# A Macaron block with tree-position attention: preparation moved out of the first rounds, into turns of 28 units, and a part of the lead given to GpSimd

## The reference

```python
q, k, v = heads(x @ Wq), heads(x @ Wk), heads(x @ Wv)        # 16 heads of 16
node_probs = softmax((x @ Wr) as (b, h, s, 4))
pos = cumsum(node_probs, axis=2) - node_probs                # in 0 .. 2047
cos, sin = tables at pos, linear between whole positions
cos_w, sin_w = sums over the 4 nodes of node_probs * cos, sin
q_r = q * cos_w + rotate_half(q) * sin_w                     # k_r likewise
scores = q_r k_r^T / 4 + log(node_probs node_probs^T + 1e-8), causal
out = softmax(scores) @ v @ Wo
```

## Time and profile before

| | |
|---|---|
| Three runs, median (lowest to highest) | 2910.24 us (2907.36 to 2912.67) |
| Profiled execution | 2896.46 us, span 2894.6 us |
| Feed-forward layer, then the lead | from 0 to 536.01 us of the span |
| Rounds 0 to 7 | 536.01 to 2529.75 us |
| Last projections, feed-forward layer | to 2894.6 us |

### The profile page before, as it was taken

One profiled execution on the slowest core, in us unless ns is written; L12 is line 12 of the kernel. 1 busy time (PEld: TensorE's weight loads), 2 busy tenths in 40 slices (PEclk: granted clock), 3 DMA queues, 4 the chain that ended last, 5 costly groups with the idle time before them and its releaser, 6 DMA issues. The chain is left out here.

```text
span 2894.6 us, 104325 instructions
## 1 busy us (share of the span) xinstructions
PE 2448.1 (85%) x45990; PEld 1896.7 (66%) x45990; DVE 1711.7 (59%) x3627; ACT 1702.9 (59%) x2174; POOL 997.9 (34%) x1497
## 2 busy tenths in 40 slices
PE   7298444587899999899999989999999999973885
PEld 4165222466788887778888777888877888841553
DVE  7732278788576567866566786666676111167431
ACT  6222123456677777667777766777776777662221
POOL 1188700334222224423222442222244222110787
PEclk9699776799999999999999999999999999986997
DMA  6555401221212112212111221211122111162565
GB/s 233 160 103 101 78 18 30 60 53 47 60 57 56 48 46 79 66 49 59 55 53 52 79 66 53 58 53 53 54 74 69 44 47 49 42 204 72 105 102 74
DMA packets 185109, 207.28 MB, mean 72 GB/s; under 512 B 35984, under 2 KB 151712, under 8 KB 184480
## 3 DMA queue, kind: packets, MB, share of 16 engines
q1 hardware_dynamic: 158880, 165.60, 19.3%
q0 software_dynamic: 24576, 34.10, 7.6%
q10 hardware_dynamic: 1152, 0.26, 0.0%
HBM read 131.68 MB, written 76.02 MB: 72 GB/s over the span
## 5 line engine op out<-in xcount | busy, mean ns | idle before, releaser
L1697 PEld LDWEIGHTS at_mix<-at_val,at_ew 128*64 128x64 f32 x34816 | 1223.7, 138 | 241.3 <-issue 36.0
L1281 ACT ACTIVATE at_ew<-at_ring 128x1024 f32<-128x1024 f32 (+1 forms) x1280 | 1124.7, 898 | 364.4 <-PE at_ring L1679 358.2
L1697 PE MATMUL at_mix<-at_val,at_ew 128*64 128x68 f32 x34816 | 1263.0, 224 | 44.7 <-DVE at_mixed L1543 28.7
L1679 PE MATMUL at_ring<-at_qT,at_kT 98*64 98x512 bf16 (+3 forms) x5120 | 698.9, 353 | 57.9 <-ACT at_ew L1281 35.8
L1202 POOL TENSOR_SCALAR_AFFINE_SELECT at_ew<-at_ew 128x256 f32<-128x256 f32 x512 | 294.3, 579 | 1074.2 <-ACT at_ew L1281 1073.5
L1543 DVE TENSOR_TENSOR at_mixed<-at_mix,at_prob 128x272 f32<-128x272 f32 x256 | 112.3, 439 | 440.4 <-PE at_mix L1697 439.1
L1679 PEld LDWEIGHTS at_ring<-at_qT,at_kT 98*64 98x64 bf16 x5120 | 228.5, 112 | 111.4 <-ACT at_ew L1281 47.6
L1224 POOL TENSOR_TENSOR at_val<-at_vo,at_val 128x256 f32<-128x256 f32 x384 | 267.4, 717 | 7.5
L344 POOL DMA_INDIRECT out_dram<-ffn_xn,ffn_idx_all x128 | 210.0, 1641 | 43.4 <-issue 35.0
L334 POOL DMA_INDIRECT ffn_xn<-table,ffn_idx_all x128 | 126.2, 986 | 278.4 <-DMA ffn_idx_all<-ffn_idx_hi 240.3
L1762 PE MATMUL at_side<-at_w_all,at_turned 128*64 128x512 f32 (+1 forms) x1024 | 197.8, 531 | 13.8 <-DVE at_bounded L1536 5.2
(11 more groups left out here) (243 smaller groups left out, 2727.1 us busy)
## 6 DMA issues: line engine op xcount, KB each, us to landing
table<-ffn_xn SPq DMA_DIRECT2D x32, 512.0 KB, 6.3
q_parts<-at_parts SPq DMA_DIRECT2D x64, 192.0 KB, 2.5
k_parts<-at_parts SPq DMA_DIRECT2D x64, 192.0 KB, 3.0
at_qT<-q_parts SPq DMA_DIRECT2D x128, 96.0 KB
at_kT<-k_parts SPq DMA_DIRECT2D x64, 192.0 KB
ffn_front<-in_L_attn_x_dram SPq DMA_DIRECT2D x16, 512.0 KB, 5.3
ffn_w_in<-in_L_ffn_w_dram SPq DMA_DIRECT2D x32, 256.0 KB, 3.6
at_xin<-out_dram SPq DMA_DIRECT2D x32, 256.0 KB, 6.0
```

The lines of the kernel that those rows point to most:

```text
L1281: act.activation(ew[u % NE_BUF][:, a:b], ring[u % 2][:, a:b], ACT.Exp).then_inc(s["exp_ready"], 1)
L1679: lastm = pe.matmul(ring[u % 2][h:h + HALF, at:at + (CH - t) * P], kT[q][:, kc + j * P + h:kc + j * P + h + HALF], qT[q][:, qc + t * P:qc ...
L1697: m = pe.matmul(mix[block_of[u] % 2][h:h + HALF, t * K * VW:(t + 1) * K * VW], ew[u % NE_BUF][:, col + h:col + h + HALF], val[q][:, tile0 ...
```

## The change

Round by round, turns are laid out anew: round 0 has four SHORT turns of 24 units; each second round has eight turns of 28 units (MID); the first rounds 2, 4 and 6 are one turn each without steps (BARE). Steps may stand at the same `at`, and VectorE's are cut into smaller ones. In MID turns ScalarE's copies stand at other distances from TensorE's steps than in LONG ones, and weighting runs without lag from 16 to 22 of a turn. Products and sums are made in quarters in MID turns. In the lead, GpSimd joins the halves and makes the product of the sine with g, and VectorE's statistics stand ahead of its positions. The rotated rows are turned by 8 transposes of whole tiles.

```diff
-    SHORT, LONG = 24, 40
-    N_SHORT = 4
+    SHORT, MID, BARE = 0, 1, 2
+    N_SHORT, N_MID = 4, 8
...
+    rounds = [first_unit[v] for v in range(V) if v == 0 or visits[v][1] != visits[v - 1][1]] + [U]
+    turns, m = [], 0
+    for r in range(len(rounds) - 1):
+        size = rounds[r + 1] - rounds[r]
+        count, kind = (N_SHORT, SHORT) if r == 0 else (N_MID, MID) if r % 2 else (1, BARE)
+        for n in range(count):
+            turns.append((rounds[r] + n * (size // count), size // count, kind, None if kind == BARE else m))
+            m += kind != BARE
...
+    STORE_AT = (20, 21, None)
...
-        BURST = 26
+        BURST, BURST_END = 16, 22
...
                 # GpSimd
-                    if at == (10 if short else 14) and new is not None:
+                    if at == (10, 12, None)[kind] and new is not None:
...
+                def join_halves(t):
+                    pool.wait_ge(s["halves_ready"], t + 1)
...
+                    pool.tensor_tensor(half(qkr, 0), half(rot_a, 0), half(rot_b, 1), ALU.subtract)
+                    pool.tensor_tensor(half(qkr, 1), half(rot_a, 1), half(rot_b, 0), ALU.add).then_inc(s["roped"], 1)
+                def sine_products(t):
+                    pool.wait_ge(s["trig_ready"], t + 1)
+                    if t > 0:
+                        pool.wait_ge(s["sq_max_ready"], t)
+                    pool.tensor_tensor(prods[:, 3, :]..., cs[:, 1, :]..., g_t..., ALU.mult).then_inc(s["g_sin_ready"], 1)
+                def lead(new, fin):
+                    if fin is not None:
+                        join_halves(fin)
+                    add_up(new)
+                    sine_products(new)
...
                 # ScalarE: turned, values, outputs, softmax, square, high, middle, low, trig, q/k, root
-                SHORT_AT = (3, 6, None, 8, 9, 12, 15, 18, 16, 23, 20)
-                LONG_AT = (4, 6, 10, 8, 16, 18, 20, 23, BURST + 2, BURST + 4, BURST + 3)
+                SHORT_AT = (3, 6, None, 8, 9, 12, 15, 19, 17, 23, 16)
+                MID_AT = (3, 5, 8, 7, 10, 14, 16, 20, 18, 25, 17)
...
                 # VectorE, lead
-                        rotate(fin)
+                        rotate(fin, 0)
+                        rotate(fin, 1, True)
                     shift_logits(new)
                     node_softmax(new)
+                    statistics(new + 1)
                     positions(new)
-                    statistics(new + 1)
...
-                    node_products(new)
-                    node_sums(0)
-                    node_sums(2)
+                    node_products(new, 0, 2)
+                    node_products(new, 2, 1)
+                    node_sums(0, 2)
+                    node_sums(2, 1)
+                    dve.wait_ge(s["g_sin_ready"], new + 1)
+                    node_sums(3, 1)
...
                 # VectorE: weights, rotate, shift, softmax, residual, positions, angles, squares, statistics,
                 # products, sums, bound, sums, normalise
-                SHORT_AT = (0, 1, 6, 8, None, 10, 12, 13, 14, 18, 19, 20, 21, 23)
-                LONG_AT = (1, 2, 5, 8, 10, 14, 17, 20, 22, 30, 32, 25, 34, 33)
+                AT = {"weights": (1, 1), "rotate": (2, 2), "rotate_2": (2, 3), "join": (3, 4), "squares": (14, 16), "bound": (20, 22),
+                      "residual": (None, 9), "shift": (6, 5), "softmax": (8, 8), "positions": (10, 11), "whole": (10, 11),
+                      "first_angles": (11, 12), "count_turns": (12, 13), "angles": (13, 13), "absolute": (13, 14),
+                      "statistics": (15, 15), "normalise": (23, 18)}
+                PRODUCTS_AT = ({18: 0, 21: 2}, {19: 0, 21: 1, 23: 2, 25: 3})
+                SUMS_AT = ({19: 0, 22: 2}, {20: 0, 22: 1, 24: 2, 26: 3})
...
                 # TensorE: inputs, values, outputs, output projection, sums, rotated, high off, middle off, squares, q/k
-                                    for h in range(0, P, HALF):
-                                        at = (g * 4 + n) * P + h
-                                        lastm = pe.matmul(side[h:h + HALF, ...], qkr[:, at:at + HALF], ident[:, :], ...)
+                                    at = (g * 4 + n) * P
+                                    lastm = pe.matmul(side[:, ...], qkr[:, at:at + P], ident[:, :], is_transpose=True, ...)
...
-                LONG_AT = (1, 3, 7, 9, 13, 15, 17, 20, 24, BURST)
+                MID_AT = (1, 3, 6, 8, 10, 12, 14, 17, 21, 23)
...
-                    if not short and (at == 0 or at >= BURST):
+                    if kind == MID and BURST <= at <= BURST_END:
                         weigh_until(u)
```

More of the change, by code:

```diff
@@ L926, in fin_of @@
     def fin_of(m):
-        return LEAD + m - 1 if LEAD + m - 1 < TP else None
+        return LEAD + m - 1 if m is not None and LEAD + m - 1 < TP else None
     with ExitStack() as ctx:
@@ L1060, in schedule @@
             first_visit()
-            for m, (start, size) in enumerate(turns):
-                for at in range(min(size, U - start)):
-                    unit(start + at, at, size == SHORT, new_of(m), fin_of(m), posts.get(m))
+            for start, size, kind, m in turns:
+                for at in range(size):
+                    unit(start + at, at, kind, new_of(m), fin_of(m), posts.get(m))
             last_projections()
@@ L1132, in first_visit, with unit @@
                     load_heads(1)
-                def unit(u, at, short, new, fin, post):
+                def unit(u, at, kind, new, fin, post):
                     if u + 2 in first_unit and u + 2 < U:
@@ L1629, in unit @@
-                    if step == 3 and new is not None:
-                        node_softmax(new)
-                    if step == 4 and post is not None:
-                        add_residual(post, 0, 1)
-                    if step == 5 and new is not None:
-                        positions(new)
-                    if step == 6 and new is not None:
-                        angles(new)
-                    if step == 7 and fin is not None:
-                        largest_squares(fin)
-                    if step == 8 and more:
-                        statistics(new + 1)
@@ L1641, in unit @@
-                    if step == 9 and new is not None:
-                        node_products(new)
-                    if step == 10 and new is not None:
-                        node_sums(0)
-                    if step == 11 and fin is not None:
-                        bound(fin)
-                    if step == 12 and new is not None:
-                        node_sums(2)
-                    if step == 13 and more:
-                        normalise(new + 1)
+                    if kind == BARE:
+                        return
@@ new lines, in unit @@
+                    step = [name for name in AT if AT[name][kind] == at]
+                    per = 2 if kind == SHORT else 1
+                    if fin is not None:
+                        if "weights" in step:
+                            turn_weights()
+                        if "rotate" in step:
+                            rotate(fin, 0)
+                        if "rotate_2" in step:
+                            rotate(fin, 1)
+                        if "join" in step:
+                            join_halves()
+                        if "squares" in step:
+                            largest_squares(fin)
+                        if "bound" in step:
+                            bound(fin)
@@ L1652, in last_projections @@
+                    if more:
+                        if "statistics" in step:
+                            statistics(new + 1)
+                        if "normalise" in step:
+                            normalise(new + 1)
                 def last_projections():
```

113 lines of the change are left out of this document (71 added, 42 removed).

## The result

The changed kernel takes 3087.03 us (median of 4 runs, 3083.77 to 3089.29), the kernel before beside it 2910.61 (2907.36 to 2912.67): a ratio of 1.0606, 95% interval 1.0588 to 1.0625. It is slower, by 176.4 us; 3080 had been forecast. The profiled execution took 3089.08 us, 3087.4 of them the span.

What follows compares the result with a forecast made beforehand. TensorE was taken to bound second rounds and idle in first rounds with preparation, VectorE to bound the lead. Sum: 2896.5 −16.5 −133 +304 +7 +17 = 3075, 3089 on the median's scale; given 3080, range 2965 to 3130.

Steps and rivals of the forecast that it cites:

- Lead: Stage ahead of the rounds: first scores come 16.5 us earlier with GpSimd's help nearly free; ends 17 and 5.
- Plain rounds: Rounds 2, 4 and 6 without steps: 107 us each, two visits taking 14.4+12.6 with a load wait; 133 us gained.
- rival C: Loads bound the plain rounds: 16 us a visit, 63 us more, 3150 in all; chance 0.07.
- Full turn: A 28-unit turn with all steps: 57.4 us, TensorE's own work plus waits and 1.7 for the clock.
- TensorE's own work: Floor of a 28-unit turn: 46.5 us, from 62.4 less 15.0 for twelve units and 0.9 for transposes.
- Copies' waits: In a 28-unit turn, TensorE waits for exponentials behind ScalarE's copies, two units behind its steps: together 4.0 us.
- Sine and cosine: In a 28-unit turn, table loads and activations keep ScalarE from exponentials: TensorE waits 3.7 us, and 0.55 two units on.
- Root: In a 28-unit turn, ScalarE's root at 17 waits for VectorE's statistics: TensorE loses 0.95 us.
- Clock: Behind the sine and cosine idling TensorE's clock falls to 1.2 GHz: 1.7 us a full turn, ends 0 and 3.
- Rounds 1, 3, 5: Second rounds of 28-unit turns: 449, 459 and 443 us, 304 lost against 1046.8.
- Round 0: Short turns where later angles and a root waiting for statistics delay sine and projection: 202 becomes 219, 17 us lost.
- Rival A: Turn stays at TensorE's work, 46.5 us, round 0 at 202: whole 2819, faster; decides below 49.9 a turn; chance 0.13.

Runs made afterwards that it cites:

- the two runs on the lead: Joins and sine product back to VectorE, on the changed kernel: ratio 1.0611; GpSimd's sine product behind VectorE's products, on the kernel with sine and cosine beside the projection: 0.9802.
- all together: Changed kernel with root and copies later, sine and cosine at 24 beside the projection, GpSimd's lead product behind VectorE's: 2836.62 us, ratio 0.9745 to the kernel before.

## Why the prediction was right

It was right in sign and size, and in mechanism for the turns, where most of the time lies; for the lead it was not. What the change touches became 175.5 us longer in the profiles (179.1 − 3.6), where the sum had 178.5. The near equality owes something to luck: the lead missed by +12.9, the plain rounds by −10.5, rounds 1, 3 and 5 by −5.9, rounds 7 and 0 by 1.3 and −1.

- **Lead**, −16.5: wrong, −3.6 (the other six kernels with this lead take 178.2 to 180.5 us, 4.3 to 6.6 less than before). The step that failed is the choice between the two ends: I took GpSimd's help as free because most of its rows beside a busy VectorE were undisturbed. The low end, 5, which has VectorE wait out what GpSimd runs, was the right one. GpSimd's own prices were well estimated: 1.26 + 1.31 for the join (2.6) and 2.35 for the product (2.6), where nothing held them. The Trainium skill (SBUF — State Buffer, section "SBUF: two separate sides") has the two engines lock each other out for a whole instruction where VectorE's has two operands in SBUF; the two runs on the lead agree, with 3.83 against 2.29 us beside a product and no change beside sums, which read one operand. Of the 13 us missing, the product (1.5) and the subtraction (1.0) make 10 over four pairs, and the first pair's second product (3.37 for 1.22) 2 more.
- **Plain rounds**, 107 each (eight visits of 13.5 are 108): 103.5. The term that was too large is the wait for a load. The load itself was well taken: the two that TensorE waits for in round 2 had been issued 14.5 and 13.7 us before, against the 14.2 of the earlier trace rows. So 14.2 us is about what such a load takes, and not a price of the stores ahead of it, as the line against rival C had it. What was wrong is the room: between the start of a load and the first scores that need it TensorE has 13.4 us of work (1229.03 to 1242.42), not 12.6, and the waits are 0.71 and 0.26 us.

```profile
1229.03 1.85 SPq L1100 DMA_DIRECT2D at_qT<-q_parts  x3
...
1242.68 0.46 PE L1753 MATMUL at_ring<-at_qT,at_kT 98*64 98x512 bf16 x4 [0.26 <-DMA at_kT<-k_parts]
```

- **Full turn**, 55.7 and 1.7 for the clock: 55.95 at a granted clock of 1.00, 57.23 with a fall. Inside, the terms moved. *TensorE's own work*, 46.5: 47.0 (busy time of the kernel with all together), 0.3 of the difference because the transposes saved 0.6 and not 0.9. *Copies' waits*, 4.0: 2.6 idle. Moving them back gave 3.86, with what each wait costs beside its idling, which I had left out; that the sum comes near 4.0 is luck. *Sine and cosine*, 3.7 and 0.55: 3.58, and 0.18 in the turn at full clock; but 1.25 of the 3.58 is the root's, and alone they cost 2.33. *Root*, 0.95: 0.88 to 1.25 for its own wait and as much again passed on to sine and cosine. The two terms together were right, their shares were not. *Clock*, 1.7: 1.28 for 3.4 us at half speed (57.23 against 55.95, two turns next to each other with the same waits but for that 0.18), and not in every turn.
- **Rounds 1, 3, 5**, 449, 459, 443: 445, 462, 437. **Round 7**, 298: 299.3, 8.4 more than before. The waits at the posts didn't come (TensorE is busy for 298.44); the two more posts make 5.1 us of busy time, and where the rest comes from was not found. **Round 0**, 219: 218, and moving the root and the two steps behind it back gives 203.8: that step was right with its cause.
- **Rival A** named 49.9 us as the turn from which the layout pays. The kernel with sine and cosine beside the projection passes it at 47.84 and comes out faster, the one with root and copies later stands on it (49.78 and 51.05) and comes out at 1.0054. In the last run rounds 1 and 3 take 370 and 378 us, near the 362 and 372 that A had from TensorE's work. So its time was right and its condition not met: the window without lag at 16 to 22 covered at most 0.6 to 1.0 us of the root's wait (1.83 without it, 0.88 to 1.25 with it).
- The advice against separating regimes that I had cited from the Trainium skill (Perfetto Trace Analysis, section "Optimization Strategy") decides nothing here: with separate regimes and other places for the steps the kernel is 2.5% faster than before.

What stays open: why the clock falls behind some waits of 1.83 to 3.58 us and not behind others of the same size. Round 0 still leaves TensorE idle for 47 to 49 of 204 us where the root stands behind sine and cosine, and for 57 to 59 of 217 where it doesn't; in the kernel after, 49 of the 57 are waits for exponentials. No run looked into them.

## What to carry to other kernels

In a loop whose order is written out, as this one, a helper engine's step costs by its place more than by its length: here it had to stand so that the main engine had a long step of its own beside it and its operand was three units old. The same work took 57 or 47 us a turn by such placing, with the window without lag and the grouping of VectorE's products moved along. When a wait is found, remove it and read the others again, because a wait hides a part of its price in the next one and in busy time. Handing work from VectorE to GpSimd paid here only where VectorE then ran instructions with one operand in SBUF.

## What the runs showed of the hardware

- VectorE's tensor_tensor with both operands in SBUF and GpSimd's tensor_tensor exclude each other: 0.29 became 1.26 us, 2.29 became 3.83, and where VectorE's started first GpSimd's 2.35 became 4.45; tensor_reduce beside the same GpSimd instruction stayed at 3.6.
- GpSimd's tensor_tensor of 128x512 takes 1.26 to 1.31 us, of 128x1024 2.35; VectorE's of 128x512 0.69, of 128x1024 1.22.
- A wait of TensorE came with about 0.28 us of busy time beside the idle time (48.34 us busy in a turn with four waits more, 47.20 without).
- Loads of 12 transfers were usable 13.7 and 14.5 us after their first issue with no store issued in the 11 us ahead of them, and 14.2 us with the lead's store ahead.
- A fall of the clock to 1.2 GHz for 3.4 us cost 1.3 us of a turn that had waits anyway (49.78 against 51.05, 55.95 against 57.23).
